# A graph-attention kernel: the rows of edge numbers come from SBUF through TensorE and PSUM, not by a broadcasting DMA for each group

## What is computed

```python
# layer 0: 4 heads of 64; weight of an edge = exp(-leaky-like(score)), summed by the edge's own node
score = own[seg] + other_term[dst] + elem * a_e + a_b          # per edge and head
num   = segment_sum(exp(clamp(score)) * feat[other], seg)      # node x 256
den   = segment_sum(exp(clamp(score)), seg)                    # node x 4
# layer 1: one head, 200 relations
score = h[src] @ w_src + h[dst] @ w_dst + rel_emb[etype] @ w_rel
alpha = exp(leaky_relu(score)); alpha = alpha / sum(alpha, axis=1)
agg   = segment_sum((h[src] + rel_emb[etype]) @ W * alpha, dst)
```

## Time and profile before

| | us |
|---|---|
| median of 3 runs | 2496.63 (2495.69 to 2500.13) |
| span of the profiled execution | 2479.6 |
| phase 0 (edge phase, l = 0) | about 258 to 950 |
| phase 1 (edge phase, l = 1) | about 1552 to 2275 |

### The profile page before, as it was taken

The page is one execution under the profiler, slowest core; times in us unless marked ns, Lnnn a source line. Parts: engine busy times, 40 slices in busy tenths (PEclk is TensorE's granted clock), DMA queues, the critical chain, the costliest instruction groups (busy, mean ns, idle before and its releaser), DMA issues. The chain is left out here.

```text
span 2479.6 us, 40282 instructions
## 1 busy us (share of the span) xinstructions
PE 1639.9 (66%) x9301; PEld 1175.0 (47%) x9301; DVE 1690.6 (68%) x4231; ACT 1080.0 (44%) x2994; POOL 1264.8 (51%) x1217
## 2 busy tenths in 40 slices
PE   0678466565666665289999956466676666766378
PEld 0576244343444444289999954233333333333266
DVE  8997766666666667677778646567777777777811
ACT  0474334443333343212222226676676676664321
POOL 0387566666666660126666610655666565652042
PEclk9889667667666666599999977566677667777689
DMA  3014444444444443289999962555665565663331
GB/s 101 2 5 68 152 107 108 109 108 110 109 108 110 107 98 67 65 281 279 301 303 303 305 213 77 172 164 160 167 165 165 161 167 162 167 169 49 91 87 22
DMA packets 212676, 351.09 MB, mean 142 GB/s; under 512 B 45840, under 2 KB 123980, under 8 KB 212588
## 3 DMA queue, kind: packets, MB, share of 16 engines
q0 software_dynamic: 75616, 167.60, 27.1%
q1 hardware_dynamic: 136972, 182.41, 23.9%
HBM read 318.55 MB, written 31.34 MB: 141 GB/s over the span
## 5 line engine op out<-in xcount | busy, mean ns | idle before, releaser
L1164 POOL DMA_INDIRECT e_rows<-table,e_gidx x880 | 846.5, 962 | 525.2 <-issue 233.1
L1227 DVE TENSOR_TENSOR acc<-acc,e_psO 128x260 f32 (+1 forms) x880 | 463.5, 527 | 274.9 <-DMA edge_rows<-row_out 156.6
L1437 PE MATMUL e_psO<-e_rows,e_oh 128*128 128x260 f32 x880 | 374.5, 594 | 233.4 <-DVE acc L1227 206.0
L1437 PEld LDWEIGHTS e_psO<-e_rows,e_oh 128*128 128x128 f32 x880 | 236.3, 290 | 314.6 <-DVE acc L1227 209.3
L2277 PE MATMUL e_psO<-e_rows,e_oh 128*128 128x456 bf16 x440 | 225.1, 512 | 95.3 <-DVE acc L1227 84.1
L1318 PE MATMUL e_psA<-e_own_of_unit,e_ohT 128*128 (+2 forms) x880 | 104.1, 184 | 188.2 <-issue 80.4
L1318 PEld LDWEIGHTS e_psA<-e_own_of_unit,e_ohT 128*128 128x128 bf16 x880 | 82.0, 103 | 274.6 <-issue 263.3
L1406 ACT ACTIVATE e_rows<-e_psA 128x16 f32<-128x16 f32 x110 | 20.3, 184 | 399.5 <-DVE e_psA L1397 300.8
L788 POOL DMA_INDIRECT records<-ordered,s_chunk x68 | 119.1, 1752 | 110.7 <-DVE s_chunk L615 80.9
L2179 ACT ACTIVATE away<-iota_b,etype 128x200 bf16<-128x200 bf16 x440 | 165.3, 446 | 0.0
L2237 DVE TENSOR_SCALAR e_oh<-iota_b,seg,inverse 128x128 bf16<-128x128 bf16 x440 | 117.9, 337 | 69.3 <-issue 57.7
(11 more groups left out here) (444 smaller groups left out, 3669.6 us busy)
## 6 DMA issues: line engine op xcount, KB each, us to landing
hot_run<-in_L_ffn_w_dram SPq DMA_DIRECT2D x107, 512.0 KB
XN<-in_L_ffn_w_dram SPq DMA_DIRECT2D x85, 512.0 KB
e_edge_row<-edge_rows SPq DMA_DIRECT2D x110, 256.0 KB
e_edge_row<-edge_rows SPq DMA_DIRECT2D x110, 128.0 KB
e_rows<-table,e_gidx POOLq DMA_INDIRECT x880
table<-frow SPq DMA_DIRECT2D x25, 192.5 KB
table<-chunk_steps SPq DMA_DIRECT2D x25, 130.0 KB, 2.2
normed_rows<-Z SPq DMA_DIRECT2D x5, 642.5 KB
```

What stands on the lines that cost most here:

```text
L1164: pool.indirect_dma_start(out=rows[:, r, t, 0:width], out_offset=None, in_=table, in_offset=bass.IndirectOffsetOnAxis(ap=gidx[:, r, t:t + ...
L1227: v.tensor_tensor(d, d, psO[:, units * (r % (4 // units)) + j, 0:accw], ALU.add).then_inc(S["added"], 1)
L1437: return pe.matmul(out[:, 0:A0], oh[:, r, t, :], rows[:, r, t, :], start=start, stop=stop)
```

## The change

The rows are loaded once, one group on each of 110 partitions (`edge_rows` in SBUF, 1 KB or 2 KB a partition). For each group PE multiplies them with a stationary matrix whose every column is the same unit vector (column g of the identity), so that all 128 partitions of a PSUM tile `row` get row g. `row` has one buffer only. DVE and ACT read it there. The PSUM bank that this costs in phase 1 is taken from `psA`, which has one buffer in place of two there. The load of W3 moves to the start of phase 0, behind the load of the rows.

```diff
-        erow = sb(tag + "edge_row", [P, DEPTH, TPG, kinds, P], BF16, c=c)
+        edge_rows = sb(tag + "edge_rows", [GROUPS[l], TPG, kinds, P], BF16, c=c)
+        row = ps(tag + "row", [P, kinds, 512], c)
-        psA = ps(tag + "psA", [P, 2, 512], c)
+        psA = ps(tag + "psA", [P, 1 if l else 2, 512], c)
+        own_banks = 1 if l else 2
...
# SP
-                    sp.dma_start(erow[:, r, :, :, :].rearrange("p t k e -> p (t k e)"),
-                                 seg_d[l][bass.ds(g * TPG, TPG), :].rearrange("t w -> (t w)").partition_broadcast(P))\
-                        .then_inc(row_landed[r], 16)
-                pipeline(sp, 0, 0, step, post.get("sync_besides", ()))
+                sp.dma_start(edge_rows[:, :, :, :].rearrange("g t k e -> g t (k e)"),
+                             seg_d[l][0:GROUPS[l] * TPG, :].rearrange("(g t) w -> g t w", t=TPG)).then_inc(rows_loaded, 16)
+                if post.get("sync_after"):
+                    post["sync_after"]()
...
# DVE, onehots (and ACT, turned_hots, alike)
-                    dve.wait_ge(row_landed[r], q * 16 + 16)
+                    dve.wait_ge(spread_ready, g + 1)
-                            ins = v.tensor_scalar(ohR[0:n, r % 2, k, :, :], erow[0:n, r, :, 1, :],
+                            ins = v.tensor_scalar(ohR[0:n, r % 2, k, :, :], row[0:n, 1, :].rearrange("p (t e) -> p t e", t=TPG),
-                        v.tensor_scalar(ohT[:, r % 2, :, :], erow[:, r, :, 0, :], unumber[:, 0:1], None, ALU.is_equal)\
+                        v.tensor_scalar(ohT[:, r % 2, :, :], row[:, 0, :].rearrange("p (t e) -> p t e", t=TPG),
+                                        unumber[:, 0:1], None, ALU.is_equal)\
...
# PE
+                pe.wait_ge(rows_loaded, 16)
+
+                def spread_row(at):
+
+                    g, q, r = at
+                    back(pe, S["ohT_ready"], g, 1)
+                    if l:
+                        back(pe, S["ohR_ready"], g, 1)
+                    hold(pe, "pe")
+                    choose = ident_b[0:GROUPS[l], bass.ds(g, 1)].to_broadcast([GROUPS[l], P])
+                    for k in range(kinds):
+                        ins = pe.matmul(row[:, k, :], choose, edge_rows[:, :, k, :], start=True, stop=True)
+                    ins.then_inc(spread_ready, 1)
 
                 def step(s, dyn):
-                    nxt, last = (locate(s, dyn, d) for d in (1, -1))
+                    soon, nxt, last = (locate(s, dyn, d) for d in (2, 1, -1))
+                    if soon is not None:
+                        spread_row(soon)
...
-                        back(pe, S["own_used"], g, 2)
+                        back(pe, S["own_used"], g, own_banks)
...
# phase 0's extras
-                            sync_besides=((1, l1_w3_load),), dve_after=l1_totals))
+                            sync_after=l1_w3_load, dve_after=l1_totals))
```

More of the change, by code:

```diff
@@ L1105, in edge_phase @@
         oh = sb(tag + "oh", [P, DEPTH, TPG, P], BF16 if l else F32, c=c)
-        erow = sb(tag + "edge_row", [P, DEPTH, TPG, kinds, P], BF16, c=c)
+        edge_rows = sb(tag + "edge_rows", [GROUPS[l], TPG, kinds, P], BF16, c=c)
+        row = ps(tag + "row", [P, kinds, 512], c)
+        spread_ready, rows_loaded = (sem(tag + n) for n in ("row_spread", "edge_rows_loaded"))
         ohR = sb(tag + "relation_hot", [P, 2, 2, TPG, P], BF16, c=c) if l else None
@@ L1123, in edge_phase @@
         fetched = [sem(tag + f"rows_landed{r}") for r in range(DEPTH)]
-        row_landed = [sem(tag + f"edge_row_landed{r}") for r in range(DEPTH)]
         chain = sem(tag + "chain")
@@ L1262, in turned_hots @@
                     g, q, r = at
-                    act.wait_ge(row_landed[r], q * 16 + 16)
+                    act.wait_ge(spread_ready, g + 1)
                     act.wait_ge(S["ohT_ready"], g)
-                    nc.scalar.activation(off_row[:, :, :], erow[:, r, :, 0, :], ACT.Abs, scale=-1.0, bias=unumber[:, 0:1])\
+                    nc.scalar.activation(off_row[:, :, :], row[:, 0, :].rearrange("p (t e) -> p t e", t=TPG), ACT.Abs, scale=-1.0, bias=unumber[:, 0:1])\
                         .then_inc(S["off_ready"], 1)
@@ L1316, in step @@
                         for t in range(TPG):
-                            out = psA[:, r % 2, t * 3 * heads:(t + 1) * 3 * heads]
+                            out = psA[:, r % own_banks, t * 3 * heads:(t + 1) * 3 * heads]
                             ins = pe.matmul(out, ohT[:, r % 2, t, :], seen[:, :, bass.ds(g * units + t // tpu, 1)]
@@ L1339, in step @@
                         ins.then_inc(S["summed"], 1)
-                pipeline(pe, 1, 1, step, post.get("pe_besides", ()))
+                pipeline(pe, 2, 1, step, post.get("pe_besides", ()))
         end_phase()
@@ L1447, in build, with l1_w3_load @@
             w3_loaded = sem("l1_w3_loaded")
-            def l1_w3_load(q, r):
+            def l1_w3_load():
                 sp = nc.sync
-                if r == 0:
-                    sp.dma_start(arow[:, :], a["L1_gnn_a"].rearrange("n o -> (n o)").partition_broadcast(P))\
-                        .then_inc(w3_loaded, 16)
-                else:
-                    at = slice((r - 1) * KD, r * KD)
+                sp.dma_start(arow[:, :], a["L1_gnn_a"].rearrange("n o -> (n o)").partition_broadcast(P))\
+                    .then_inc(w3_loaded, 16)
+                for j in range(3):
+                    at = slice(j * KD, (j + 1) * KD)
                     sp.dma_start(w3r[:, at, :], a["L1_gnn_W3"].rearrange("(j p) n -> p j n", p=P)[:, at, :])\
@@ L2191, in l1_own @@
                 dve.wait_ge(S["own_e"], g + 1)
-                v.tensor_reduce(mine[:, r % 2, :], psA[:, r % 2, 0:TPG * 3].rearrange("p (t j) -> p t j", t=TPG),
+                v.tensor_reduce(mine[:, r % 2, :], psA[:, 0, 0:TPG * 3].rearrange("p (t j) -> p t j", t=TPG),
                                 AX.X, ALU.add).then_inc(S["own_used"], 1)
```

## The result

| | before | changed |
|---|---|---|
| median of 12 runs, us | 2497.32 (2493.78 to 2500.32) | 2501.65 (2496.54 to 2510.61) |
| span of the profiled execution, us | 2479.6 | 2508.3 |

The ratio is 1.0026, 95% interval 1.0014 to 1.0037: slower by 6.5 us (3.5 to 9.2; the medians differ by 4.3), where 15 us were forecast. The two profiles alone would say 28.7 us. That they say so much more than the medians is the first thing to explain.

The account below looks back on a forecast made before the run. It took late signals of PE's products, for which POOL, DVE and PE wait (the stall), as the bound. Phase 0: 0, phase 1: +14, starts: +2 us, on span 2479.6 plus 17.0, gave 2512 us; range 2455 to 2580, likeliest 2502 to 2536.

Parts of the forecast that it names:

- The base of the sum: Phase 1 of the kernel before was taken at 6.35 us a group, a mix of stretches of eight and four gathers.
- The long form mostly turns into the short form: Phase 1: POOL's pauses after eight gathers mostly become pauses after four, 6.50 us a group against 6.35, +14 us.
- The starts: Start of each phase: row and one-hot run in single file, about +1 us each, +2 us in all.
- Phase 0: nothing: Phase 0: DVE's longer read and PE's matmul fall where these engines wait, so the change costs 0.
- Rival D: Phase 0: POOL pauses after every four gathers too, +62 us, 2574 us in all; chance 0.06.
- SP's loads: Missing broadcast loads: worth zero in phase 0, 0.16 us less for each stall in phase 1 (bounds 0 and 0.48).
- Rival C: Both phases: the stall hangs on the broadcasts and goes with them, 120 and 73 us less, 2304 us; chance 0.09.
- rival B: The stall shortens with the traffic: 26 us less in phase 1, 8 us in phase 0, 2463 us; chance 0.22.
- Rival E: Neither does anything measurable: the row is not on the path and phase 1 keeps its mix, 2497 us; chance 0.14.
- DVE's read from PSUM: DVE's comparisons of the fp32 row take 684 ns each: +0.28 us a group in phase 0, +0.66 us in phase 1.
- Rival A: Phase 1: DVE becomes the bound, 73 us more, 2570 us, or 2535 if in half of the steps; chance 0.17.
- Gathers beside a comparison: POOL's gathers next to a DVE comparison last 0.94 to 0.95 us as any other, so nothing was added.

Follow-up runs that it names:

- before_again: The kernel before, run again without any edit, on a pausing chip: ratio 1.0008, phase 0 679.7 us, phase 1 716.0 us.
- after_third: The changed kernel run again without any edit, on a steady chip: ratio 1.0223 to the kernel before there, phase 1 608.8 us.
- one_bank: The kernel before with one buffer of `psA` in place of two in phase 1, on a steady chip: ratio 0.9997.
- phase0_only: The kernel before with the change in phase 0 only, phase 1 as before, on a pausing chip: ratio 0.9997.
- after_again: The changed kernel run again without any edit, on a pausing chip: ratio 1.0039 to the kernel before there.
- spread_unread_2: The kernel before with one buffer of `psA` and PE's two row matmuls a group, read by nobody, in phase 1, on a steady chip: phase 1 561 us.

## Why the prediction was right in direction and wrong in size

The measured change, +6.5 us by the ratio and +4.3 us by the medians, is well under the +15 us forecast. Two steps of the sum failed, and one small term was mis-sized the other way.

*The base of the sum.* This step failed first. "The mean of 6.35 is a mix" took the mix of one execution for the kernel's own. The usual one is 6.51 us a group (716.0 / 110), so that "Against 6.35 that is +0.15 x 110" compared a forecast of the changed kernel with an unusual execution of before. On the right base the same working, 6.50 against 6.51 us, would have given nothing. A warning lay in front of me: I put the 17.0 us by which the span was under the median down to "what lies around the span". A run of the changed kernel of 2510.21 us has a span of 2508.3, so 1.9 us lie around it, and the profiled execution of before was 15 to 16 us quicker than usual.

*"The long form mostly turns into the short form."* This step failed too. 28 stretches of eight and 42 of four in before_again are 26 and 46 in the changed kernel, and half of the groups are still in stretches of eight. The 0.4 us of room that DVE's 0.66 and PE's 0.4 us were to use up is not used up: in stretches of eight the first product ends 3.32 us after the restart in the changed kernel and 3.35 us in before_again (medians). DVE and PE wait behind each pause anyway, and PE's granted clock is higher (a product of phase 1 takes 3.12 us in place of 3.41); how much each of the two does isn't told apart. Nor is the end of that product what decides: of the 77 products of phase 1 of before_again whose signal can be matched, 41 are signalled over 1 us late although their matmuls end within 4.7 us of a restart. What decides is not known. That 6.50 us a group were forecast and 6.55 measured (720.2 / 110) is luck: the forecast had stretches of four alone, at 6.66 - 0.16; measured are a mix of 12.69 / 2 = 6.35 and 6.73 us.

*The starts.* I gave them +1 us each. Measured are 3.5 to 3.8 us in phase 1 where POOL pauses, and 1.3 to 2.4 us in phase 0, together some 5 to 6 us, most of the change. The working had only the single file of row and one-hot in it. On a steady chip that is about right for phase 1 (to the 25th gather 32.0 us in after_third, 31.0 in one_bank). It put the one bank of `psA` at "about 0.2 us after L1200", and so left out that DVE's own sum may itself wait for a held signal; there the bank keeps PE's product back, and the first pause grows by 3 us.

*Phase 0: nothing.* Right within the noise: phase0_only 0.9997. The pause there is 3.62 us in the changed kernel and 3.66 in before_again (medians), so the 3.49 of the earlier trace rows was of that execution too. Rival D is out with it: 44 stretches of eight gathers in phase 0 of the changed kernel, 3 of four.

*SP's loads.* The value that I took, 0.16 us for each pause of phase 1, is not borne out: the median pause after eight gathers, from start to start, is 3.94 us in the changed kernel and 3.77 in before_again. The end of phase 0 had the right answer, that of phase 1 the wrong one. Rival C is out: the stall stays with no broadcast in flight. For rival B nothing speaks: no pause got shorter by more than 0.04 us.

*Rival E*, that neither does anything that can be measured and "phase 1 keeps its mix", comes nearest to what happened, with its chance of 0.14; it missed only the starts. The direction was forecast rightly, but from a base that was wrong, so that this too is in good part luck.

*DVE's read from PSUM.* The mechanism was right and the term too small: 0.66 us a group forecast, 0.77 measured; L1864's 684 ns was no upper bound. By the Trainium skill, VectorE: DVE Perf Modes (section "Why PSUM operands drop a tier"), an fp32 operand in PSUM leaves one element a cycle. The direction agrees with 740 ns against 353; the estimate of 658 ns worked out from its figures falls short by 82 ns.

*PE.* 472 ns for a matmul in the mean, between my 0.22 and 0.63. The low bound was too low: at the clock's upper level it takes 375 to 389 ns, not half of the 587 to 635 ns at the lower one. One bank of psA costs nothing on a steady chip.

*Rival A*, DVE as the bound of phase 1: not on the pausing chips, where DVE waits behind each pause and takes the 85 us (0.77 x 110) of added work nearly whole into its idle time. On steady chips it is the whole result, 50 us: 5.56 us a step against a forecast of 5.69.

*Gathers beside a comparison.* I wrote that such a gather lasts "0.94 to 0.95 us as any other". That is wrong for phase 1. In before_again 43 of the 44 gathers of phase 1 that took over 1.0 us overlap one of DVE's two comparisons; in the changed kernel one gather takes over 1.0 us, and not beside a comparison. Not every overlap does it: 128 gathers of that phase overlap one. The shown profile has it too (37 of 38). One of before_again's, behind the comparison that it overlaps:

```profile
1714.11 0.61 DVE L1200 TENSOR_SCALAR e_relation_hot<-e_edge_row,unumber 128x512 bf16<-128x512 bf16 x2
...
1714.43 1.10 POOL L1164 DMA_INDIRECT e_rows<-table,e_gidx  x1 [0.30 <-issue]
```

This is what the Trainium skill says on the page SBUF — State Buffer (section "Who interferes with whom"): a VectorE instruction in one of the modes that use both ports, which a tensor_scalar can enter, shuts GpSimd out of the pair that they share, and one outside these modes with at most one input in SBUF doesn't. The trace agrees as far as the times go; which mode an instruction ran in it doesn't tell. The price is small, 0.16 us for each of 43 gathers, 7 us of POOL's time, and it counts only where POOL is the bound.

*What stays open.* Why the two kinds of chips differ; what holds PE's signal on the pausing ones, and what decides between eight and four gathers; whether the single bank of `psA` alone gives the 3 us at the start of phase 1, which only a run of one_bank on a pausing chip would show; and why the ratios there (0.35 to 0.43%, 9 to 11 us) say more than the 4 to 6 us of phase 1 in the traces.

## What to carry to other kernels

Set the profile's span beside the median before you build a sum on the profile: where it lies further off than a run's own overhead, the pattern that you read in it may be that of a rare execution, and the usual one has to be seen first. Work that is moved onto an engine is free only as long as that engine waits for something else: here DVE's 0.77 us a group, and PE's matmuls with it, cost at most 0.02 us a group behind the first six groups where a stall covered them (0.6 to 2.1 us over 104 groups), and 0.45 us where it didn't. Look at the first groups of a loop by themselves: a buffer fewer can cost nothing in the steady part and 3 us once, where a late signal meets it. A stall whose cause the trace doesn't show may be the chip's and not the kernel's, so price a change also for the case that it is gone.

## What the runs showed of the hardware

Four chips of one kind ran the same kernel in 2500 us (two of them) and in 2225 us (two), 12% apart. Nearly the whole difference lies in the two phases in which POOL issues gathers: 680 and 716 us in before_again, against 554 and 561 in one_bank, which takes as long as the kernel before there. On a pausing chip the signals that PE sends with its matmuls can be held. In phase 0 of after_again (300 to 900 us) 84 of those whose record is there are recorded within 0.3 us, and all 84 matmuls end within 4.7 us of POOL's restart; 144 are recorded late, and all but one of these end 6.4 us or more after it, the records coming together 2.7 to 2.9 us after the start of the last gather (the last packet of the gathers ends at 526.81 us, the records follow at 527.09 to 527.21). In phase 1 there is no such bound: of 82 signals of a product there 41 are recorded over 1 us late although their matmuls end within 4.7 us of a restart. DVE's signals are not held: in phase 0 of the changed kernel (300 to 900 us) all 574 with a record come within 0.3 us, in the middle of a stall too (own sum of 508.58 to 508.78 us, recorded at 508.80). On a steady chip 469 of 473 of PE's signals (spread_unread_2, 400 to 800 and 1500 to 2000 us) are recorded within 0.3 us. A comparison of 512 columns took 740 ns from fp32 in PSUM and 350 ns from bf16 in SBUF, while ACT's operation on them was quicker from PSUM (672 against 713 ns).
